# A four-layer graph network on one core: features loaded first in six pieces, zero matmuls at the start, and first-layer work moved to GpSimd and ScalarE

## The reference, cut to what matters

```python
def _L0_gnn_ref(x, support, weight):
    bw = _bin_sign(weight)
    ba = _bin_sign_z(x)
    xw = ba @ bw.T
    out = support @ xw
    return jax.nn.relu(out)
...
x = _layernorm(x + _L0_gnn_ref(x, adj, L0_gnn_weight), axis=-1)
x = _layernorm(x + _L1_gnn_ref(x, adj, adj, ...), axis=-1)
x = _layernorm(x + _L2_gnn_ref(x, adj, L2_gnn_W, L2_gnn_b), axis=-1)
x = _layernorm(x + _L3_gnn_ref(x, adj, L3_gnn_W_stack), axis=-1)
```

## Time and profile before

| what | value |
|---|---|
| median of 3 runs | 487.82 us (487.76 to 487.89) |
| the profiled execution, its own time | 489.84 us |
| its span, first to last instruction | 488.0 us |
| PE busy | 471.8 us (97%) |
| DVE busy | 353.9 us (73%) |
| ACT busy | 231.5 us (47%) |
| POOL busy | 176.6 us (36%) |
| mean granted TensorE clock | 0.998 |

### The profile page before, as it was taken

The page is one execution under the profiler, slowest core; times in us unless marked ns, Lnnn a source line. Parts: engine busy times, 40 slices in busy tenths (PEclk is TensorE's granted clock), DMA queues, the critical chain, the costliest instruction groups (busy, mean ns, idle before and its releaser), DMA issues. The chain is left out here.

```text
span 488.0 us, 5657 instructions
## 1 busy us (share of the span) xinstructions
PE 471.8 (97%) x1903; PEld 310.2 (64%) x1903; DVE 353.9 (73%) x766; ACT 231.5 (47%) x404; POOL 176.6 (36%) x175
## 2 busy tenths in 40 slices
PE   5989999999999999999999999999999999999994
PEld 4989955455555578887544444554556645878882
DVE  4589889999984599839332963892853299699994
ACT  5666529991877653333333631351342366343200
POOL 1412152461523138934100631460431055356641
PEclk9999999999999999999999999999999999999999
DMA  8775130000354100000000000000000000000001
GB/s 295 231 231 159 41 116 0 0 0 1 114 193 150 33 1 1 0 1 1 1 0 0 0 1 0 1 1 0 1 0 1 0 1 1 0 12 21 24 21 38
DMA packets 8147, 20.67 MB, mean 42 GB/s; under 512 B 976, under 2 KB 4708, under 8 KB 8120
## 3 DMA queue, kind: packets, MB, share of 16 engines
q1 hardware_dynamic: 6840, 18.75, 11.7%
q0 software_dynamic: 464, 0.79, 0.9%
q10 hardware_dynamic: 816, 0.79, 0.5%
HBM read 18.94 MB, written 1.39 MB: 42 GB/s over the span
## 5 line engine op out<-in xcount | busy, mean ns | idle before, releaser
L1450 PE MATMUL psum<-QT,xT 128*128 128x512 f32 (+3 forms) x264 | 108.5, 542 | 0.0
L412 POOL TENSOR_TENSOR es<-es,ST 128x512 f32<-128x512 f32 (+3 forms) x60 | 75.0, 1251 | 51.2 <-ACT ST L606 49.5
L601 ACT ACTIVATE ST<-psum 128x512 f32<-128x512 f32 (+3 forms) x66 | 36.1, 547 | 86.8 <-DVE rm L951 77.6
L1450 PEld LDWEIGHTS psum<-QT,xT 128*128 128x128 f32 (+1 forms) x264 | 47.7, 186 | 40.4 <-issue 34.0
L951 DVE TENSOR_TENSOR rm<-psum,rm 128x512 f32<-128x512 f32 (+3 forms) x60 | 37.4, 624 | 38.7 <-PE psum L1450 38.4
L362 POOL TENSOR_TENSOR rstd<-veps,nhalf 128x1 f32<-128x1 f32 (+1 forms) x44 | 29.9, 679 | 87.9 <-DVE veps L743 87.8
L1564 PE MATMUL psum<-Wh,ST 128*128 128x256 f32 (+3 forms) x242 | 55.1, 380 | 0.0
L1494 PE MATMUL psum<-ST,Wh 128*128 128x512 f32 (+3 forms) x132 | 54.5, 542 | 0.0
L1262 PE MATMUL psum<-eb,x_all 128*128 128x512 f32 (+3 forms) x132 | 51.9, 542 | 0.0
L606 ACT ACTIVATE ST<-ST 128x512 f32<-128x512 f32 (+3 forms) x66 | 37.9, 579 | 28.3 <-DVE ST L973 25.7
L1226 PE MATMUL psum<-adjT,x_all 128*128 128x512 f32 (+3 forms) x132 | 50.4, 542 | 0.0
(11 more groups left out here) (166 smaller groups left out, 762.5 us busy)
## 6 DMA issues: line engine op xcount, KB each, us to landing
adj_rows<-in_adj_dram SPq DMA_DIRECT2D x10, 677.0 KB, 5.1
rows<-in_adj_dram SPq DMA_DIRECT2D x10, 677.0 KB, 4.0
out_dram<-xs SPq DMA_DIRECT2D x10, 128.0 KB, 1.7
x_all<-in_x_dram SPq DMA_DIRECT2D x2, 512.0 KB, 6.7
W<-in_L_gnn_W_stack_dram SPq DMA_DIRECT2D x2, 512.0 KB, 5.7
adj_rows<-in_adj_dram SPq DMA_DIRECT2D x1, 338.5 KB
rows<-in_adj_dram SPq DMA_DIRECT2D x1, 338.5 KB
w0n<-in_L_gnn_weight_dram ACTq DMA_DIRECT2D x1, 256.0 KB, 5.1
```

The lines of the kernel that those rows point to most:

```text
L412: nc.gpsimd.tensor_tensor(es[0:r, g % 2, 0:w], es[0:r, g % 2, 0:w], buf(g)[0:r, j, 0:w], ALU.add)\
L601: nc.scalar.activation(buf(g)[0:r, j, 0:w], psum[0:r, SB[n % 3], 0:w], ACT.Copy).then_inc(st_ready.sem, 1)
L1450: last = nc.tensor.matmul(psum[0:r, SB[n % 3], 0:w], xT[l][:, k, j * P:j * P + r], QT[:, k, c0:c1], start=(k == 0), stop=(k == KD - 1))
```

## The change

All of it is in the first layer.

- **Loads.** SP loads `w0` first, then `x` in five pieces of two tiles and the tail, and only then the row tiles of `adj` in order.
- **Zeros.** DVE's first instruction zeroes a block of `dots`; PE multiplies it with itself nine times into a bank that nobody reads.
- **Head.** `w0`, the transposes of `pos` and the products go pair by pair of tiles (six pairs); `adj_turn(0)` comes after all of them. ACT copies four pairs of both, DVE two.
- **`lo`.** DVE makes groups 0 and 1, POOL group 2 (`low_group`), 3 of 11 blocks. `agg_a(i)` now waits for each group where it needs it. In the last tile the splits and transposes take 74 columns instead of 128.
- **Norm.** DVE computes only minus mean times root (`shift_a`, one column); ACT applies scale and shift (`apply_a`), for tile i - 2 behind its copies of tile i.
- **POOL's list.** `low_group` stands between the `rsqrt`s; the ten small loads that came before them come behind the last.

```diff
+    WARM = 9
+    LOW = 2
...
-            load_rows(0)
-            for g in range(BANKS_T):
...
+            sp.dma_start(w0n[:, :, :], w0.rearrange("(k p) d -> p k d", p=P)).then_inc(w0_in.sem, 16)
+            for n in range(PAIRS - 1):
+                sp.dma_start(x_all[:, 2 * n:2 * n + 2, :], x[2 * n * P:(2 * n + 2) * P, :].rearrange("(t p) d -> p t d", p=P))\
+                    .then_inc(x_in[n].sem, 16)
...
+            for i in range(FULL):
                 load_rows(i)
...
+            def low_group(i):
+
+                pool.wait_ge(adjT_banks_read.sem, BANKS_T * (i + 1))
+                r = kk(i)
+                k0, k1 = grp(LOW)
+                nc.gpsimd.tensor_tensor(lo[:, i % PARTS, k0:k1, 0:r], adjT[:, k0:k1, i * P:i * P + r], hi[:, i % PARTS, k0:k1, 0:r],
+                                        ALU.subtract).then_inc(lo_ready_pool.sem, 1)
+
+            low_group(0)
             pool.dma_start(a_b[:, :], a_sa.partition_broadcast(P).rearrange("p a d -> p (a d)")).then_inc(a_in.sem, 16)
-            pool.wait_ge(adjT_turned.sem, 2 * BANKS_T)
+            low_group(1)
...
+            for i in range(T):
+                rsqrt(NA, i)
+                if i + 2 < T:
+                    low_group(i + 2)
...
+            def apply_a(i):
+                r = kk(i)
+                act.wait_ge(nmr_ready.sem, i + 1)
+                nc.scalar.activation(x_all[0:r, i, :], vbuf[0:r, i % 4, :], ACT.Identity, bias=nmr[0:r, i % 4, :],
+                                     scale=rstd[0:r, i % 4, :]).then_inc(NA.x_ready.sem, 1)
+
             for i in range(1, T):
                 adj_evac(i)
+                if i >= 2:
+                    apply_a(i - 2)
...
+            nc.vector.memset(dots[:, 0, 0:P], 0.0).then_inc(zeros_ready.sem, 1)
...
+            def shift_a(i):
+                r = kk(i)
+                dve.wait_ge(NA.rstd_ready.sem, i + 1)
+                nc.vector.scalar_tensor_tensor(out=nmr[0:r, i % 4, :], in0=mv[0:r, i % 4, 0:1], scalar=-1.0, in1=rstd[0:r, i % 4, :],
+                                               op0=ALU.mult, op1=ALU.mult).then_inc(nmr_ready.sem, 1)
...
-                norm_apply(NA, i, vbuf[0:kk(i), i % 4, :])
+                shift_a(i)
                 if i + 2 < T:
-                    lower_bits(i + 2, range(1, BANKS_T))
+                    lower_bits(i + 2, range(1, LOW))
...
+            pe.wait_ge(zeros_ready.sem, 1)
+            for _ in range(WARM):
+                nc.tensor.matmul(bank(7, 0, P), dots[:, 0, 0:P], dots[:, 0, 0:P], start=True, stop=True)
             pe.wait_ge(ident_ready.sem, 2)
...
+            turn_x(0)
+            turn_x(1)
+            turn_x(2)
             mul_pos(0)
-            turn_pos(2)
+            turn_x(3)
             mul_pos(1)
+            turn_x(4)
             mul_pos(2)
+            turn_x(5)
+            mul_pos(3)
+            mul_pos(4)
+            mul_pos(5)
+            pe.wait_ge(pads_zero.sem, 1)
+            adj_turn(0)
             adj_turn(1)
...
             def agg_a(i):
                 r = kk(i)
-                pe.wait_ge(lo_ready.sem, i + 1)
...
                 for k in range(T):
+                    if k < LOW * EB and k % EB == 0:
+                        pe.wait_ge(lo_ready.sem, i * LOW + k // EB + 1)
+                    if k == LOW * EB:
+                        pe.wait_ge(lo_ready_pool.sem, i + 1)
```

More of the change, by code:

```diff
@@ L431, in _, with adj_evac @@
             own = Own(act, act_own.sem)
[L432 to L434 removed]
+            def adj_evac(i, groups=range(BANKS_T)):
+                r = kk(i)
                 if i >= PARTS:
                     act.wait_ge(agga_done.sem, i - PARTS + 1)
[L437 removed]
+                for g in groups:
                     k0, k1 = grp(g)
                     act.wait_ge(adjT_turned.sem, i * BANKS_T + g + 1)
[L440 to L444, removed]
+                    src = bank((i % 2) * BANKS_T + g, 0, (k1 - k0) * P).rearrange("p (k n) -> p k n", n=P)[:, :, 0:r]
+                    nc.scalar.activation(adjT[:, k0:k1, i * P:i * P + r], src, ACT.Copy)
+                    nc.scalar.activation(hi[:, i % PARTS, k0:k1, 0:r], src, ACT.Copy).then_inc(adjT_banks_read.sem, 1)
             act.wait_ge(w0T_ps.sem, 1)
@@ L1142, in adj_turn, with copied, turn_x, mul_pos @@
                     for k in range(k0, k1):
-                        last = nc.tensor.transpose(bank((i % 2) * BANKS_T + g, (k - k0) * P, (k - k0 + 1) * P),
-                                                   adj_rows[:, i % 3, k * P:(k + 1) * P], ident[:, :])
+                        c = (k - k0) * P
+                        last = nc.tensor.transpose(bank((i % 2) * BANKS_T + g, c, c + r), adj_rows[0:r, i % 3, k * P:(k + 1) * P],
+                                                   ident[0:r, 0:r])
                     last.then_inc(adjT_turned.sem, 1)
-            pe.wait_ge(pads_zero.sem, 1)
-            adj_turn(0)
+            def copied(n):
+                if n < 4:
+                    pe.wait_ge(posT_ready_act.sem, n + 1)
+                else:
+                    pe.wait_ge(posT_ready.sem, n - 3)
+            def turn_x(n):
+                t0, t1 = 2 * n, min(2 * n + 2, T)
+                pe.wait_ge(pos_ready.sem, n + 1)
+                if n >= 3:
+                    copied(n - 3)
+                for k in range(KD):
+                    for t in range(t0, t1):
+                        c = (k * (t1 - t0) + t - t0) * P
+                        last = nc.tensor.transpose(bankb(n % 3)[:, c:c + P], pos[:, t, k * P:(k + 1) * P], identb[:, :])
+                last.then_inc(pos_ps.sem, 1)
+            def mul_pos(n):
+                t0, t1 = 2 * n, min(2 * n + 2, T)
+                if n == 0:
+                    pe.wait_ge(w0T_ready.sem, 1)
+                if n == 5:
+                    pe.wait_ge(xw_ready_act.sem, 1)
+                copied(n)
+                for t in range(t0, t1):
+                    for k in range(KD):
+                        last = nc.tensor.matmul(bank(XW[n], (t % 2) * D, (t % 2 + 1) * D), posT[:, k, t * P:(t + 1) * P],
+                                                w0T[:, k, :], start=(k == 0), stop=(k == KD - 1))
+                last.then_inc(xw_ps.sem, 1)
             pe.wait_ge(w0_signed.sem, 1)
```

131 lines of the change are left out of this document (56 added, 75 removed).

## The result

| | before | changed |
|---|---|---|
| median | 487.86 us (487.76 to 488.17, 6 runs) | 484.03 us (483.51 to 484.59, 6 runs) |
| the profiled execution, its own time | 489.84 us | 483.51 us |
| its span | 488.0 us | 481.7 us |

The ratio is 0.9921, with a 95% interval of 0.9909 to 0.9934: faster by 3.8 us, where 6.5 us was forecast. The two profiled executions are 6.3 us apart, close to the forecast's sum, and the medians are not. Most of this text is on that difference. Part of the closeness is luck: 483.51 us is the lowest of the changed kernel's 16 timed executions.

A forecast was written before the change was run, and what follows sets the result against it. PE was taken to bound the kernel, busy nearly throughout from 5.33 us. Head 3.7, row tiles 2.6 and last tile 0.2 us sum to 6.5 us, so 487.82 us becomes 481.3 us (480.0 to 482.6, wider to 484.8).

The forecast's parts named there:

- the head's gain: First layer's start, until row tile 2's transposes: `agg_a(0)` ends near 15.9 us instead of 19.57, 3.7 us gained.
- a second total: End time: 6.5 us off the profiled execution's 489.84 us gives 483.3 us, beside 481.3 us from the median.
- the walk through the head: Head, part by part: loads, zeros, copies and transposes timed until `agg_a(0)` ends near 15.9 us.
- The row tiles: First layer from 19.57 to 60.26 us: PE's waits for `lo` vanish, 2.6 us gained, bounds 0 and 2.6.
- the last tile: Last row tile: eleven transposes of 74 instead of 128 columns give 0.2 us, between 0 and 0.5.
- DVE and POOL holding each other up: Row tiles: POOL's `lo` delays DVE; under 1 us lost, or about 494 us at worst; chances 0.07 and 0.03.
- The clock that falls back: Head: PE waits for `x` and drops to 1.2 GHz; 2.3 us less gain, 483.6 us; chance 0.15.
- Late row tiles: Head: row tile 1 of `adj` lands near 14 us; head gives 1.7 us, 483.3 us; chance 0.08.
- Zeros without effect: Head bound by PE at 1.2 GHz, `agg_a(0)` ends near 19 us; 484.5 us; chance 0.07.
- the wider range: Total time: up to 484.8 us, taking in the clock, the late tiles and the zeros.
- The forecast's own range: Total time: 480.0 to 482.6 us, from handoffs between engines and 0 to 0.5 us of the last tile.

The follow-up runs named there:

- head_alone: Changed kernel with all `lo` and the norm back on DVE, and the load of `a_b` held until row tile 0 is copied: 485.13 us, ratio 0.9938.
- apply_dve: Changed kernel with the norm applied by DVE again, the third of `lo` staying on POOL: 486.24 us, ratio 0.9961.
- head_only: Changed kernel with all `lo` and the norm back on DVE, the load of `a_b` not held and issued at 1.91 us: 488.87 us, ratio 1.0012.
- lo_dve_again: Second timing of the changed kernel with group 2 of `lo` back on DVE and the norm on ACT: 483.84 us, ratio 0.9912.
- after_again: The changed kernel timed once more, no edit, beside the kernel before: 485.08 us, ratio 0.9936.
- before_again: The kernel before timed once more, no edit: 487.98 us (487.81 to 489.75, 12 runs).
- tiles_only: The kernel before with its old head, plus split `lo`, norm on ACT, waits by group, late small loads and narrow last tile: 486.21 us, ratio 0.9956.
- no_zeros: The changed kernel without the nine products of zeros, nothing else: 485.30 us, ratio 0.9943.

## Why the prediction was right in direction and 2.7 us off in size

**Which execution the sum was made on.** This is the step that failed. The prediction took the head's gain, 3.7 us, from row tile 2 at 19.57 us, and of the 2.0 us that the profiled execution took over the median it made only a second total (483.3 us beside 481.3). Those 2.0 us lay in the head itself (2.08 us by the traces): the usual execution turns row tile 2 at 17.49 us. Three profiles of the changed kernel turn it at 16.34, 16.91 and 17.25 us, so the head gives 0.2 to 1.2 us against the usual execution, not 3.7. Against the profiled one it gave 3.2 us: the walk through the head was good (15.9 forecast, 16.34 measured), its base was not. The sum was then subtracted from a median in which the 2 us had never been. With 3.1 us of the row tiles, 0.2 to 1.2 us of head make 3.4 to 4.3 us; the medians gave 3.8, 2.9 and 3.0 us. The two lower ones hold the five executions with the lower granted clock.

**The row tiles.** 2.6 + 0.2 us were forecast and 3.12 us measured (40.69 to 37.57). The waits went to nothing; the last tile gave 0.5 instead of 0.2, the upper of its bounds (transposes 0.87 against 1.36 us). But the cause was half wrong: the prediction let DVE lose 0.55 us a round by POOL's `lo` and 0.41 by the norm. Among the four kernels with the new head only the norm counts (38.80 to 37.49); the `lo` on POOL counts nothing (38.80 to 38.89). The other 1.88 us, 40.68 to 38.80, come with the parts that head_alone keeps: 0.5 from the narrow tile, the rest from waits by group, the small loads behind the `rstd`s and the new head, which were not tried apart.

**The rivals.** DVE and POOL holding each other up was judged from the dot products to cost a share of POOL's time, with DVE's full delay as the worst case. The full delay is what apply_dve shows where they meet: 0.41 us became 1.10. It did not cost the changed kernel anything, because DVE with the norm gone has the room: 31.15 us busy of 37.57. The Trainium skill ("SBUF — State Buffer", Who interferes with whom) has the rule in that form: for a DVE instruction with two SBUF inputs or in a two-port mode, whoever starts second is blocked for the other's whole instruction. Which of these the norm is, no run shows. The traces agree, with 1.09 us of POOL and 1.10 us of DVE, and the forecast should have used it in full. The clock that falls back exists, but was seen only in head_only's profile, behind a pause of 2.24 us; whether it is what the changed kernel's five slowest executions had stays open. A clock that rises late in spite of the zeros (lo_dve_again, 1.25 us) was no rival of the prediction. Late row tiles exist too (after_again, 0.9 us). Zeros without effect is wrong for the profiles and nearly right for the median.

**The bounds.** 484.03 us lies inside the wider range, up to 484.8 us, held by the rivals for the clock and the loads. That is in part luck: the range had room for a late clock in the changed kernel, not for a base that was 2 us too slow. The forecast's own range, 480.0 to 482.6 us, was too narrow: handoffs between engines were its only spread, and the executions of one kernel differ by 2 us in the head.

**The change without the third on POOL.** lo_dve, the change without `low_group`, took 483.84 us both times. Against the changed kernel timed beside it (484.93 us) that is 1.1 us less, with intervals that just meet (0.9897 to 0.9926 and 0.9926 to 0.9951). The row tiles account for 0.08 us of it; whether the rest is more than the head's scatter stays open.

## What to carry to other kernels

Before a profile becomes the base of a sum, compare its own time with the median: if they differ, find the stretch in which the difference lies, since a gain there may exist in that execution alone. Work moved from DVE to POOL can leave DVE's busy time as it was (35.58 and 35.69 us here); look at DVE's busy column after the move, and try ACT, which took the norm here without a wait of PE. When an engine's first instruction is taken away, see what stands behind it: a load freed early can cost more than the instruction did.

## What the runs showed of the hardware

**POOL can hold a DVE instruction for a whole series.** In the changed kernel DVE's mask of one input, 0.86 us in the median, once started beside eleven instructions of POOL in a row and lasted nearly as long as they did. A one-column operation, 0.15 us in the median, once took about as long as a `lo` on POOL:

```profile
61.50 4.69 POOL L385 TENSOR_SCALAR xp<-x_all 128x256 f32<-128x256 f32 x11
61.51 4.43 DVE L846 TENSOR_SCALAR eb<-adjT 128x1354 f32<-128x1354 f32 x1
```

```profile
29.18 0.99 POOL L354 TENSOR_TENSOR lo<-adjT,hi 128x384 fp32r<-128x384 f32 x1
29.24 0.95 DVE L790 SCALAR_TENSOR_TENSOR nmr<-mv,rstd 128x1 f32<-128x1 f32 x1 [0.44 <-POOL rstd L365]
```

**Transposes alone took TensorE to its higher level.** In before_again no product of the kernel had run before 10.54 us, yet the eight transposes at 9.56 us take 0.62 us where the eight at 8.06 us take 0.93. In tiles_only eight transposes at 8.18 us take 0.70 us, also ahead of any product. It does not happen each time: in the execution of the forecast the same transposes ran and the level stayed low into the products. The forecast had weighed a rule of the Trainium skill ("TensorE: Matmul & The Clock Gate", Part 4: PE-mode transpose) that transposes do not count as work for the clock; these two traces speak against it.

**The level rises at very different times.** Of the ten profiles with zeros first, nine have it up before 7 us and one (lo_dve_again) after 10 us; in the four without, it rises between 8 and 15 us (before_again, tiles_only, no_zeros, and the execution of the forecast as the last). It can also fall again: in head_only it was up at 5.03 us, PE then paused 2.24 and 1.24 us with four transposes of 0.46 us between, and the granted clock was 0.51 from 10 to 15 us.

**One kernel's loads at the start differ by a microsecond.** In one execution of the changed kernel row tile 0 of `adj` was there when PE came for it at 10.89 us; in two others PE waited for it until 11.44 and 11.78 us.
